# A two-layer graph network on one core: the first stage counts only totals, and the prefixes are counted inside the sort, in one PSUM bank

## What is computed

```python
h = relu(layernorm(x)) @ W                    # 4 heads of 32
alpha = leaky_relu(s_src[src] + s_dst[dst])   # s_*: h times the two halves of att
ex = exp(alpha - m[src])                      # softmax over the edges of one src node
x = x + segment_sum(ex / denom[src] * h[dst], dst) + bias
h = relu(layernorm(x))
msg = relu(concat(h[src], h[dst], edge_attr) @ W1 + b1) @ W2 + b2
x = x + segment_sum(msg, src)
```

## Time and profile before

| | |
|---|---|
| median of 3 runs | 5412.68 us (5402.25 to 5417.56) |
| the profiled execution | 5404.83 us, span 5403.0 us |
| first stage, to the sort's first instruction on DVE | 0 to 297.1 us |
| sort, first to last indirect DMA | 316.3 to 2330.5 us |

### The profile page before, as it was taken

One profiled execution on the slowest core, in us unless ns is written; L12 is line 12 of the kernel. 1 busy time (PEld: TensorE's weight loads), 2 busy tenths in 40 slices (PEclk: granted clock), 3 DMA queues, 4 the chain that ended last, 5 costly groups with the idle time before them and its releaser, 6 DMA issues. The chain is left out here.

```text
span 5403.0 us, 98958 instructions
## 1 busy us (share of the span) xinstructions
PE 4070.9 (75%) x22798; PEld 3396.3 (63%) x22799; DVE 3569.6 (66%) x8071; ACT 3043.6 (56%) x4591; POOL 3250.7 (60%) x3487
## 2 busy tenths in 40 slices
PE   5778777777777777700799987777777777777778
PEld 5766666666666666600799965666666666666666
DVE  8945444444444444429999986777777777777776
ACT  5545555555555555401677756666666666666665
POOL 2357777777777777750000005777777777777774
PEclk9988888888888888855899999999999999999999
DMA  8865555555555554597200046656666666666655
GB/s 311 321 204 151 139 139 140 140 139 141 139 140 142 139 139 139 156 89 19 58 0 0 0 114 162 147 144 147 144 148 144 147 144 147 144 147 144 147 144 134
DMA packets 1212202, 734.52 MB, mean 136 GB/s; under 512 B 929642, under 2 KB 1031204, under 8 KB 1205388
## 3 DMA queue, kind: packets, MB, share of 16 engines
q1 hardware_dynamic: 862700, 336.19, 31.5%
q0 software_dynamic: 131424, 275.52, 17.5%
q10 hardware_dynamic: 218048, 122.49, 7.6%
HBM read 562.32 MB, written 165.09 MB: 135 GB/s over the span
## 5 line engine op out<-in xcount | busy, mean ns | idle before, releaser
L1086 POOL DMA_INDIRECT g_q<-q_d,g_aux x1660 | 1571.3, 947 | 1380.3 <-DMA pw<-g_q 874.7
L577 POOL DMA_INDIRECT rec_d<-rec,place x1568 | 1536.3, 980 | 502.8 <-issue 476.1
L1393 PE MATMUL g_hp<-pw,g_mix 128*128 x3328 | 878.1, 386 | 317.0 <-ACT g_mix L1290 310.8
L690 PE MATMUL lk<-tab_sd,low 128*128 128x196 f32 x3136 | 1050.8, 422 | 0.0
L1404 PE MATMUL g_ap<-g_hid,g_oh 128*128 128x256 f32 x3328 | 876.4, 386 | 133.9 <-DVE agg L1196 129.7
L626 DVE TENSOR_REDUCE rank<-equal 128x4 f32<-128x512 bf16 x392 | 262.4, 684 | 1015.4 <-ACT equal L554 1014.8
L1310 ACT ACTIVATE g_hid<-g_q 128x512 f32<-128x512 f32 x832 | 524.0, 630 | 712.5 <-DVE g_q L1182 699.2
L1393 PEld LDWEIGHTS g_hp<-pw,g_mix 128*128 128x128 f32 x3328 | 617.2, 190 | 475.2 <-issue 399.3
L1182 DVE TENSOR_TENSOR g_q<-g_hp,g_q 128x512 f32<-128x512 f32 x832 | 573.2, 689 | 484.9 <-DMA g_q<-q_d,g_aux 333.9
L687 PE MATMUL lk<-mask,hx 122*128 122x245 bf16 x1568 | 480.0, 306 | 440.2 <-ACT low L543 440.2
L554 ACT ACTIVATE equal<-rk,minus_two 128x512 bf16<-128x512 f32 x392 | 261.5, 685 | 958.9 <-DMA rec_d<-rec,place 643.1
(11 more groups left out here) (251 smaller groups left out, 5035.2 us busy)
## 6 DMA issues: line engine op xcount, KB each, us to landing
low_row<-rows_d SPq DMA_DIRECT2D x392, 256.0 KB
rec_d<-pad ACTq DMA_DIRECT2D x49, 1152.0 KB, 4.3
g_ea<-rec_d SPq DMA_DIRECT2D x208, 256.0 KB, 4.2
rec<-in_ea ACTq DMA_DIRECT2D x196, 256.0 KB
hx_row<-rows_d SPq DMA_DIRECT2D x392, 98.0 KB
g_lrow<-low_row_d SPq DMA_DIRECT2D x208, 128.0 KB, 4.2
g_q<-q_d,g_aux POOLq DMA_INDIRECT x1660, 3.0
rec_d<-rec,place POOLq DMA_INDIRECT x1568
```

The costliest lines, as they stand in the source:

```text
L577: pool.indirect_dma_start(rec_d, bass.IndirectOffsetOnAxis(ap=place[0:n, at, j:j + 1], axis=0), rec[0:n, at, j, :], None).then_inc(s_sc[at ...
L690: mm = pe.matmul(to[:, NB:LK], low[:, par, 1, slots], tab_sd[:, :, :].rearrange("p h a -> p (h a)"), start=False, stop=True, skip_group_ch ...
L1086: pool.indirect_dma_start(qg[:, par, j, :], None, q_d, bass.IndirectOffsetOnAxis(ap=aux[:, par, j, F_IDX - F_LOW:REC - F_LOW].bitcast(I32) ...
L1393: mm = pe.matmul(hp[u][:, k * HID:(k + 1) * HID], mix[:, par, 2 * u + k, :], pw[:, bass.ds(b[k], 1), :].rearrange("p o f -> p (o f)"), sta ...
```

## The change

- The first stage counts totals only. DVE makes the one-hots of four groups with two instructions (4096 and 1568 columns, two buffers), PE multiplies them in 32 products of 49 columns each that all add into one strip of one bank (`cnt[:, PRE:PRE + NB]`), two rounds ahead of the node block's work. Gone are ACT's four copies a step, the four stores of prefixes, POOL's sums and `pre_d`, `pre_in`, `tot`.
- The first two rounds of one-hots are made right behind the source digits.
- The prefixes are counted in the sort: DVE `onehots(g)` makes the two one-hots of one group (1024 and 392 columns), comparing the digits with the numbers 0 to 127 that now lie as f32 in a PSUM bank (`digits`), and PE `counted(g + 1)` stands between `matched` 0 and `looked` 0 of group g. `table` reads the prefixes from the bank `cnt`, and PE counts the next group only when `table` has read the last.
- SP loads six rows a group; the loads of groups 0 and 1 are issued in the first stage, behind the store of `rows`.
- `sums` shares a bank with `lk[0]`; `deg` is read from `cnt`. `FILL` is 26: 64 padding stores of 936 KB, 15 of them early on SP.

```diff
-FILL = 32
+FILL = 26
@@ first stage, DVE
+                    def onehots(it, par):
+                        if not first(it, 2):
+                            v.wait_ge(s_hist, it - 1)
+                        of = low_src[:, bass.ds(it * FOUR, FOUR), :]
+                        v.tensor_tensor(oh_low[:, par, :, :, :], of.unsqueeze(2).to_broadcast([P, FOUR, P, G]),
+                                        iota_g[:, :, :].unsqueeze(1).to_broadcast([P, FOUR, P, G]), ALU.is_equal)
+                        of = high_src[:, bass.ds(it * FOUR, FOUR), :].rearrange("p k j -> p (k j)")
+                        v.tensor_tensor(oh_high[:, par, :, :, :].rearrange("p k j a -> p (k j) a"), col(of, P, FOUR * G, NB),
+                                        row(iota_b[:, 0:NB], P, FOUR * G, NB), ALU.is_equal).then_inc(s_oh1, 1)
+                    v.wait_ge(s_dig, 2)
+                    onehots(0, 0)
+                    onehots(1, 1)
                     v.wait_ge(s_flat, 16)
@@ first stage, PE
+                    def count(it, par):
+                        pe.wait_ge(s_oh1, it + 1)
+                        for k in range(FOUR):
+                            for j in range(G):
+                                mm = pe.matmul(cnt[:, PRE:PRE + NB], oh_low[:, par, k, :, j], oh_high[:, par, k, j, :],
+                                               start=first(it) and k == 0 and j == 0,
+                                               stop=isinstance(it, int) and it == NB - 1 and k == FOUR - 1 and j == G - 1,
+                                               skip_group_check=True)
                         mm.then_inc(s_hist, 1)
@@ step, PE
                         pe.transpose(tp[:, 0:P], hb[:, :], ident[:, :]).then_inc(s_t, 1)
-                        count(it * FOUR, 0)
-                        count(it * FOUR + 1, 1)
+                        if not last:
+                            count(it + 2, par)
                         pe.wait_ge(s_hT, it + 1)
...
-                        count(it * FOUR + 2, 2)
-                        count(it * FOUR + 3, 3)
@@ sort, DVE
+                    def onehots(g, par):
+                        if not first(g, 2):
+                            v.wait_ge(s_cnt, g - 1)
+                        tile = lambda a: a[:, bass.ds(g, 1), :].rearrange("p o j -> p (o j)")
+                        v.tensor_tensor(ohl[:, par, :, :], row(tile(low_src), P, P, G), col(digits, P, P, G), ALU.is_equal)
+                        v.tensor_tensor(ohh[:, par, :, :], col(tile(high_src), P, G, NB), row(digits[:, 0:NB], P, G, NB),
+                                        ALU.is_equal).then_inc(s_oh, 1)
+                    onehots(0, 0)
+                    onehots(1, 1)
@@ table
-                        v.tensor_tensor(tab[:, par, :, :], pre_in[:, par, :].rearrange("p (j a) -> p j a", j=G),
+                        v.wait_ge(s_cnt, g + 1)
+                        v.tensor_tensor(tab[:, par, :, :], cnt[:, 0:PRE].rearrange("p (j a) -> p j a", j=G),
@@
                             prepare(i * DEEP + (k + 1), (k + 1) % 2)
+                            onehots(i * DEEP + (k + 2), k % 2)
                             finish(i * DEEP + k, k)
@@ sort, PE
+                    def counted(g, par):
+                        pe.wait_ge(s_oh, g + 1)
+                        if not first(g):
+                            pe.wait_ge(s_tab, g)
+                        for j in range(G):
+                            mm = pe.matmul(cnt[:, j * NB:PRE], ohl[:, par, :, j], row(ohh[:, par, j, :], P, G - j, NB),
+                                           start=(j == 0), stop=(j == G - 1), skip_group_check=True)
+                        mm.then_inc(s_cnt, 1)
+
+                    def group(g, par, last=False):
                         pe.wait_ge(s_hx, g + 1)
                         matched(g, par, 0)
+                        if not last:
+                            counted(g + 1, 1 - par)
                         pe.wait_ge(s_low, g + 1)
```

More of the change, by code:

```diff
@@ L211, in build @@
                 pick = sb("pick", [P, NB], F32, ctx)
[L212 to L217, removed]
+                oh_low = sb("oh_low", [P, 2, FOUR, P, G], BF16, ctx)
+                oh_high = sb("oh_high", [P, 2, FOUR, G, NB], BF16, ctx)
                 tp, mp = pb("l0_tp", ctx), pb("l0_mp", ctx)
@@ L246, in store @@
                     def store(it):
[L247 to L250, removed]
                         sp.wait_ge(s_ev, it + 1)
@@ L256, in _ @@
                     sp.dma_start(rows_d.rearrange("r (p c) -> p r c", p=P), rows[:, :, :]).then_inc(s_rowst, 16)
+                    sp.wait_ge(s_rowst, 16)
+                    load_group(sp, 0, 0)
+                    load_group(sp, 1, 1)
                     with sp.Fori(0, NB) as it:
                         store(it)
[L259 to L263, removed]
                     sp.wait_ge(s_hs, 16 * NB)
@@ L375, in _, with step @@
                                            op0=ALU.mult, op1=ALU.mult).then_inc(s_rstd, 1)
[L376 to L380 removed]
+                    with v.Fori(1, NB // 2) as i:
+                        onehots(i * 2, 0)
+                        onehots(i * 2 + 1, 1)
+                    onehots(NB - 1, 0)
                 @block.tensor
                 def _(pe):
[L384 to L391 removed]
+                    def count(it, par):
[6 more added lines that the diff above has]
+                                               skip_group_check=True)
                         mm.then_inc(s_hist, 1)
[L394 removed]
+                    def step(it, par, last=False):
                         pe.wait_ge(s_h, it + 1)
@@ L404, in step @@
                         pe.matmul(mp[:, 0:D + 2 * HEADS], hT[:, :], wx[:, :], start=True, stop=True).then_inc(s_mm, 1)
-                        count(it * FOUR + 2, 2)
-                        count(it * FOUR + 3, 3)
+                    count(0, 0)
+                    count(1, 1)
                     pe.wait_ge(s_wx, 1)
-                    step(0)
-                    with pe.Fori(1, NB) as it:
-                        step(it)
+                    pairs(pe, step, NB - 3)
+                    step(NB - 3, 0)
+                    step(NB - 2, 1, last=True)
+                    step(NB - 1, 0, last=True)
                 @block.scalar
@@ L709, in _ @@
                                   ).then_inc(s_sum, 1)
-                    pairs(pe, group, NG)
+                    counted(0, 0)
+                    pairs(pe, group, NG - 2)
+                    group(NG - 2, 0)
+                    group(NG - 1, 1, last=True)
         S = TILES
```

85 lines of the change are left out of this document (22 added, 63 removed).

## The result

The changed kernel takes **5335.6 us** (5330.6 to 5335.7, four runs) against 5414.0 (5402.3 to 5417.6, four runs): a ratio of 0.9857, 95% interval 0.9845 to 0.9870. That is 78.4 us less by the medians, where 62.8 were forecast. The profiled executions took 5404.8 and 5330.6 us, with spans of 5403.0 and 5328.7; the second is the lowest of its kernel's four, 5 us under the other three.

| stretch | before | after | difference | forecast |
|---|---|---|---|---|
| start to the sort's first DVE instruction | 297.1 | 240.5 | -56.6 | -54.3 |
| from there to POOL's first scatter | 19.2 | 19.3 | +0.1 | +1.5 |
| first to last scatter | 2014.3 | 1993.7 | -20.6 | -10 |
| the rest | 3072.4 | 3075.2 | +2.8 | 0 |

What follows compares the result with a forecast made beforehand. DVE was taken to pace the first stage and POOL the sort. -54.3 + 1.5 + 0 - 10 = -62.8 us from 5408.7 gave 5346 us; own range 5328 to 5362, with rivals 5325 to 5376.

Steps and rivals of the forecast that it cites:

- The first stage: Stage ahead of the sort: steps of four groups fall from 5.1 to 4.0 us, sort begins 54.3 us earlier.
- rival 3: First stage: the four-group one-hot loses its two-column rate, a step takes 6.2 us; 5449 us, slower; chance 0.04.
- The bound of -69 us: First stage: largest gain allowed, at 3.8 us a step, if an instruction's fixed part is larger than read.
- PE's product of 49 columns: First stage's counting: 0.043 us a product, 1.4 us for 32, PE busy 2.2 of 4.0 us a step.
- Rival 1: First stage gains less: steps of 4.32 us or more, or early padding stores delay the loop; 5361 to 5371; chance 0.12.
- The start of the sort: Extra one-hots and counting ahead of the sort's first scatter: +1.5 us, range 0 to 4.
- A group of the sort: Added DVE and PE work in each sort group hides under POOL's 10.2 us: cost 0.
- rival 5: Sort: a group's turn outgrows POOL, counting late or at 1.2 GHz, 11.5 us a turn; 5600 us; chance 0.05.
- The cover of 0.4 us a group: Sort: margin of a group's turn under POOL's 10.2 us; each 0.1 us beyond it costs 20 us.
- rival 4: Sort: new one-hots hold POOL up despite a PSUM operand; 5375 or 5600 us; chance 0.05, half of it slower.
- Rival 2: Sort: POOL is not relieved, everything else as forecast; 5356 us; chance 0.08.
- POOL: Sort's scatters: `table` reading one operand from PSUM shortens late entries, -10 us, range 0 to -15.

Runs made afterwards that it cites:

- high_packed: Changed kernel with the first stage's high one-hot laid out like the low one, the group's eight places innermost: 5320.0 us.
- psum_sum: Changed kernel plus an unused DVE addition of 392 f32 columns in each sort group, one operand in PSUM: 5341.3 us.
- count_twice: Changed kernel with PE doing the eight products of each sort group's prefixes twice, same values: 5334.7 us.
- sbuf_numbers: Changed kernel with the sort's one-hots comparing with bf16 numbers in SBUF instead of f32 numbers in PSUM: 5387.3 us.
- two_sbuf_sum: Changed kernel plus an unused DVE addition of 392 f32 columns in each sort group, both operands in SBUF: 5341.8 us.
- second pair: The kernel before and the changed kernel, both unedited, each profiled once more: 5411.0 and 5330.2 us.

## Why the prediction was right, point by point

**The first stage** was right by its own steps. The loop started at 43.28 (43.7 forecast). The one-hots take 2.28 and 1.78 us (2.24 and 1.72) and start 3.90 us apart (3.96, rounded to 4.0), so two columns in 1.065 ns and 0.06 us fixed hold for a four-group instruction, and rival 3 is refuted. The bound of -69 us was added up wrongly: a step of 3.8 gives -64 by the prediction's own working. The last one-hot ends at 226.87 instead of 231.7, of which 47 x 0.1 = 4.7 us is the rounding. The way from there to the sort was 13.7 us and not 11.1: the last two blocks and the round's counting take longer than the same stretch of before. The two errors cancel in part. PE's product of 49 columns is a term that was mis-sized: 0.067 us, not 0.043, and PE is busy for 2.9 us of a step (137.99 us over 47), not 2.2. It lies in PE's wait for DVE, so it cost nothing here, and it was the limit at once in high_packed, where it was 0.100. Rival 1 is refuted too: DVE's idle time is 0.2 us, at 303 GB/s; the padding stores keep nobody waiting.

**The start of the sort** cost 0.1 us, not 1.5. `looked` starts 9.0 us behind the stage's start, 1.1 later than before (1.6 were forecast), and what follows takes 1.0 us less.

**A group of the sort.** The cost of 0 was right, and rival 5 is refuted, by psum_sum on DVE and by count_twice on PE. POOL has 476.3 us of "issue" after, 476.1 before, and waits for `place` only 1.3 us beyond the first one.

The cover of 0.4 us a group was read wrongly, though. The turn of 9.7 us in the earlier trace rows holds a stretch at the lower clock: the granted clock from 356.64 to 366.36 is 0.82. Two turns later, ACT in the kernel before, and the window of that turn:

```profile
375.55 0.67 ACT L554 ACTIVATE equal<-rk,minus_two 128x512 bf16<-128x512 f32 x1
...
383.61 0.67 ACT L554 ACTIVATE equal<-rk,minus_two 128x512 bf16<-128x512 f32 x1
```

```profile
375.55:383.61 8.06, 6.40 (x50) 5.45 (x50) 4.88 (x15) 5.15 (x5) 5.92 (x8) 1.00 0.64 174
```

The same in an early group of the kernel after:

```profile
297.05 0.66 ACT L525 ACTIVATE equal<-rk,minus_two 128x512 bf16<-128x512 f32 x1
...
305.12 0.67 ACT L525 ACTIVATE equal<-rk,minus_two 128x512 bf16<-128x512 f32 x1
```

```profile
297.05:305.12 8.07, 7.17 (x57) 6.30 (x58) 6.38 (x15) 5.15 (x6) 6.23 (x7) 1.00 0.61 162
```

A turn at the full clock takes 8.1 us in both, and 8.1 also in count_twice (303.45 to 311.53). So `counted` adds nothing to it: it lies wholly in PE's idle time, and the cover is 2.1 us at the full clock. The sort's granted clock is 0.89 where it was 0.83, as said ("above 0.83"). PE's idle time ahead of `looked` did not go away altogether, as I had said it nearly would: the page has 440.2 us before and 174.8 after, and the timeline of a group still shows 0.59.

```profile
L687 PE MATMUL lk<-mask,hx 122*128 122x245 bf16 x1568 | 480.0, 306 | 440.2 <-ACT low L543 440.2
L673 PE MATMUL lk<-mask,hx 122*128 122x245 bf16 x1568 | 457.9, 292 | 174.8 <-ACT low L514 174.8
```

**The new one-hots** hold POOL up by nothing, with one operand in PSUM, and rival 4 is refuted: the excess fell. sbuf_numbers shows that it was the operand in PSUM that did it, at a price of 57 us otherwise. Rival 2 is refuted as well: no late entry lies beside `table` any more, and two_sbuf_sum brings them back.

**POOL** is where the sum was off: -20.6 us against -10. The mechanism was right, and so was the size that was costed. The relief by `table` was 11.2 us by the late entries of the trace, and 9.5 to 13 by two_sbuf_sum. But two things weren't in the step. The excess beside `hx`, which it took as given, rose from 3.2 to 7.1 us (3.9 to 4.9 in the second pair), so that the excess as a whole fell by 6 to 12 us. And the median entry fell by 9 ns, 14 us in 1568 entries, which is repeatable and not explained. Without these 14 us the two profiled executions would differ by 60 us, where 62.8 were forecast.

The Trainium skill's rule (SBUF — State Buffer, "SBUF: two separate sides") has a VectorE instruction with two SBUF inputs keep GpSimd off SBUF for its whole length. The trace bears it out, for the 0.56 us of `table` as for the 6.7 us of the long sum: the entry that meets one is held until it ends. The prediction had found that it fails for line 617, because it charged 76% of each instruction's length, 83 us in all. That isn't what the rows give. Entries start every 1.27 us, and only a start in the first 0.43 us of a `table` costs anything, half of that on average: 0.43 x 0.43 / (2 x 1.27) = 0.07 us for each, 14 us at most for 196, an estimate from the earlier trace rows and the table of ends. 11.2 and 12.7 were measured. With one operand in PSUM the loss is gone in every case.

## What to carry to other kernels

Where GpSimd issues the DMAs and sets the pace, look at the slack of VectorE beside it: one operand in PSUM was worth more than VectorE's faster pace, even where it made the instruction two and a half times as long (0.49 to 1.22 us here). Price a collision by where it falls: the entry that meets the instruction loses all that is left of it, and the others nothing, so by that reading one long instruction costs more than several short ones of the same total length. Ask of a shortened or restrided operand what it does to the engine that reads it: the packed one-hot saved DVE 0.8 us a step and cost PE 1.1. Read a serial engine's time as a median times a count and an excess: 4 ns in the median of 1568 entries are 6 us, as much as many of the edits in question. Look first whether the same engine's untouched instructions moved as well, and repeat the pair. And before a turn is compared with a bound, read the clock that was granted in it: 9.7 us here were 8.1 at the full clock.

## What the runs showed that I had not expected

- The median time of an indirect DMA's entry on POOL takes one of a few values, 958, 962 or 967 ns, for the same instruction with the same data. 967 and 958 came back when their kernels ran again. In the four executions with 962 POOL's other entries are slower as well, and none of those was repeated. No cause was found.
- A moving operand with a stride of eight bf16 elements makes a product of 49 columns take 0.100 us instead of 0.067.
- A late entry is held until the VectorE instruction beside it ends, and only if it starts while that instruction runs. Of 196 sums of `table`, 51 made one late.
- `hx`, which reads one tensor and a scalar for each partition, holds POOL up as well: the entry beside it takes 1.16 us instead of 0.96, and with its digit in PSUM no excess is left.
- Twice the counting on PE raised the granted clock of the sort from 0.89 to 0.92 and cost no time.
